# The last two row tiles' transposes on the DMA queue, and a group copy ahead of the seventh exponential, in a GroupNorm attention kernel

## What is computed

```python
h = group_norm(x, gn_w, gn_b); hf = h.reshape(B, C, H * W)        # (8, 128, 1024)
q = einsum('bcn,oc->bno', hf, wq) + bq
k = einsum('bcn,oc->bon', hf, wk) + bk[None, :, None]
v = einsum('bcn,oc->bno', hf, wv) + bv
alpha = softmax(einsum('bnc,bcm->bnm', q, k) / sqrt(C), axis=-1)   # (8, 1024, 1024)
out = einsum('bnm,bmc->bnc', alpha, v)
out = einsum('bnc,oc->bon', out, wo) + bo[None, :, None]
return out.reshape(x.shape) + x
```

## Time and profile before

| | us |
|---|---|
| median of 3 runs | 223.59 |
| lowest and highest | 222.37, 223.93 |
| the profiled execution | 222.1 |
| its span | 220.4 |
| TensorE busy (matmuls) | 203.2 |
| VectorE busy | 180.9 |
| ScalarE busy | 177.3 |
| GpSimd busy | 166.3 |

### The profile page before, as it was taken

The page is one execution under the profiler, slowest core; times in us unless marked ns, Lnnn a source line. Parts: engine busy times, 40 slices in busy tenths (PEclk is TensorE's granted clock), DMA queues, the critical chain, the costliest instruction groups (busy, mean ns, idle before and its releaser), DMA issues.

```text
span 220.4 us, 4306 instructions
## 1 busy us (share of the span) xinstructions
PE 203.2 (92%) x1513; PEld 139.9 (63%) x1513; DVE 180.9 (82%) x277; ACT 177.3 (80%) x279; POOL 166.3 (75%) x233
## 2 busy tenths in 40 slices
PE   0898679999999999999999999999999989998993
PEld 0764236767576756767576766667576657765993
DVE  1788999988889887989889897989877887788642
ACT  2259989998888889888998699888998888888820
POOL 6039996876889979997889949999689986795500
PEclk9999999999999999999999999999999999999999
DMA  5790999999999999999999999999999999999981
GB/s 160 231 400 18 190 161 225 188 179 226 201 204 195 229 171 212 247 178 189 202 174 249 187 224 212 229 174 223 209 171 219 182 227 196 187 192 205 276 304 51
DMA packets 135029, 44.61 MB, mean 202 GB/s; under 512 B 131168, under 2 KB 131936, under 8 KB 135008
## 3 DMA queue, kind: packets, MB, share of 16 engines
q1 hardware_dynamic: 134432, 44.08, 102.0%
q10 hardware_dynamic: 576, 0.26, 0.4%
HBM read 7.61 MB, written 4.22 MB: 54 GB/s over the span
## 4 chain that ended last, share of the span: by engine, by line
PE 75%; DVE 9%; issue 8%; ACT 5%; DMA 2%; SPq 0%; ACTq 0%; DVEq 0%
PE O L601 11%; PE O L603 10%; PE O L602 10%; PE S L570 10%; PE S L574 10%; PE S L572 10%; DVE neg_logits L911 5%; PE M L467 3%; PE M L466 3%; PE M L468 3%; DVE parts L927 2%; DMA x_sb<-in_x_dram 2%; ACT S L779 2%; ACT av L759 2%; ACT parts L790 1%
## 5 line engine op out<-in xcount | busy, mean ns | idle before, releaser
L911 DVE TENSOR_SCALAR_CACHE_REDUCE neg_logits<-S,c_tok 128x1024 f32<-128x1024 f32 x64 | 81.9, 1280 | 22.7 <-PE S L574 22.4
L779 ACT ACTIVATE S<-neg_logits,exp_bias 128x1024 f32<-128x1024 f32 x64 | 71.6, 1118 | 17.9 <-DVE neg_logits L911 17.7
L927 DVE SCALAR_TENSOR_TENSOR parts<-S,parts 128x1024 f16<-128x1024 f32 x64 | 78.0, 1219 | 1.7 <-ACT parts L790 1.3
L601 PE MATMUL O<-pT,v_hi 128*128 128x256 f16 x240 | 65.3, 272 | 3.7 <-ACT av L759 3.7
L790 ACT ACTIVATE parts<-S 128x1024 f16<-128x1024 f32 x64 | 65.4, 1022 | 1.6
L603 PE MATMUL O<-pT,v_lo 128*128 128x256 f16 x240 | 65.4, 272 | 0.0
L602 PE MATMUL O<-pT,v_hi 128*128 128x256 f16 x240 | 65.4, 272 | 0.0
L570 PE MATMUL S<-h_hi,u_hi 128*128 128x512 f16 x128 | 38.1, 379 | 2.4 <-DVE parts L927 2.4
L574 PE MATMUL S<-h_hi,u_lo 128*128 128x512 f16 x128 | 38.1, 379 | 0.0
L572 PE MATMUL S<-h_lo,u_hi 128*128 128x512 f16 x128 | 38.1, 379 | 0.0
L601 PEld LDWEIGHTS O<-pT,v_hi 128*128 128x128 f16 x240 | 24.3, 101 | 11.2 <-issue 4.9
(11 more groups left out here) (148 smaller groups left out, 287.4 us busy)
## 6 DMA issues: line engine op xcount, KB each, us to landing
x_sb<-in_x_dram SPq DMA_DIRECT2D x7, 512.0 KB, 8.4
inv_rows<-inv_line SPq DMA_DIRECT2D x6, 512.0 KB, 4.8
out_dram<-x_sb SPq DMA_DIRECT2D x6, 512.0 KB, 3.8
pT<-parts SPq DMA_TRANSPOSE x62, 4.8
out_dram<-x_sb SPq DMA_DIRECT2D x3, 256.0 KB, 4.7
x_sb<-in_x_dram SPq DMA_DIRECT2D x2, 256.0 KB, 3.9
out_dram<-x_sb SPq DMA_DIRECT2D x2, 128.0 KB, 1.9
inv_line<-row_inv SPq DMA_DIRECT2D x6, 4.0 KB, 2.0
```

The lines of the kernel that those rows point to most:

```text
L601: nc.tensor.matmul(o, vh, ph, start=(m == 0), stop=False)
L779: nc.scalar.activation(S[T % 3][:, :], neg_logits[:, n % 2, :], ACT.Exp, scale=-1.0, bias=exp_bias[:, p, n:n + 1], accum_out=row_sum[:, p, ...
L911: nc.vector.tensor_scalar(neg_logits[:, n % 2, :], S[T % 3][:, :], c_tok[:, p, n:n + 1], None, ALU.add, ALU.min, accum_out=exp_bias[:, p, ...
L927: nc.vector.scalar_tensor_tensor(out=parts[:, T % SPLITS, N:2 * N], in0=S[T % 3][:, :], scalar=P_SCALE, in1=parts[:, T % SPLITS, 0:N], op0 ...
```

## The change

Two things. First, `transpose` is issued for all 64 tiles; `last_transpose` on TensorE, the copies behind it on ScalarE and VectorE and their semaphores go, and each half of `last_values` waits for the DMA transposes of its two tiles. Second, at n = 6 ScalarE's copy of the group sums moves from behind the tile's exponentials to ahead of them.

```diff
@@ sync
             for b in range(B):
                 for n in range(TILES):
-                    if TILES * b + n < LAST_TILES[0]:
-                        transpose(b, n)
+                    transpose(b, n)
@@ tensor: last_values
                 if half == 0:
                     pe.wait_ge(inv_out, I0 + 3)
-                    for t in range(GT // 2):
-                        pe.wait_ge(tr_in[GT + t], 16 * B)
                 else:
                     pe.wait_ge(lo_done, TILES * B - 2)
-                    pe.wait_ge(last_tr_hi, 2)
-                    pe.wait_ge(last_tr_lo, 2)
+                for t in range(GT // 2):
+                    pe.wait_ge(tr_in[GT + 2 * half + t], 16 * B)
@@ tensor
-            def last_transpose(T):
-                pe.wait_ge(lo_done, T + 1)
-                for m in range(2 * TILES):
-                    done = nc.tensor.transpose(S[T % 3][:, :].bitcast(fp16)[:, m * 128:(m + 1) * 128],
-                                               parts[:, T % SPLITS, m * 128:(m + 1) * 128], ident16[:, :])
-                done.then_inc(last_tr, 1)
@@ tensor: behind the loop
                 if n == 1:
                     spread_inverse(I0 + 2, 1, B - 1, 0)
-                    last_transpose(LAST_TILES[0])
                 if n == 2:
-                    last_transpose(LAST_TILES[1])
                     spread_inverse(I0 + 3, 2, B - 1, 1)
                 values(*unit_of(B, n))
@@ scalar
+                    if n == 6 and b >= 1:
+                        copy_values(b - 1, 1)
                     exponentials(b, n)
                     if n == 2 and b >= 1:
                         copy_values(b - 1, 0)
-                    if n == 6 and b >= 1:
-                        copy_values(b - 1, 1)
                     high_part(b, n)
             copy_inverses(I0 + 2)
-            for i, T in enumerate(LAST_TILES):
-                act.wait_ge(last_tr, i + 1)
-                nc.scalar.copy(last_pT(T)[:, 0:TILES, :], ...).then_inc(last_tr_hi, 1)
             copy_inverses(I0 + 3)
@@ vector
-            for i, T in enumerate(LAST_TILES):
-                dve.wait_ge(last_tr, i + 1)
-                nc.vector.tensor_copy(last_pT(T)[:, TILES:2 * TILES, :], ...).then_inc(last_tr_lo, 1)
```

More of the change, by code:

```diff
@@ L120, in groupnorm_attention_kernel @@
         ident_ready = sem("ident_ready")
-        last_tr, last_tr_hi, last_tr_lo = sem("last_tr"), sem("last_tr_hi"), sem("last_tr_lo")
         a_mm, small_mm, ob_mm, woT_mm, b_mm = (
@@ L178, in groupnorm_attention_kernel @@
         I0 = 0
-        LAST_TILES = (TILES * B - 2, TILES * B - 1)
         LAST = (slice(0, GT // 2), slice(GT // 2, GT))
@@ L191, in groupnorm_attention_kernel @@
         LAST_INV = last_inv[:, 2:4, :].rearrange("c q n -> c (q n)")
-        def last_pT(T):
-            return pT[:, T // GT % PT, :, T % GT, :]
         def unit_of(b, n):
@@ L837, in _ @@
                         copy_values(b - 1, 0)
-                    if n == 6 and b >= 1:
-                        copy_values(b - 1, 1)
                     high_part(b, n)
             copy_inverses(I0 + 2)
-            for i, T in enumerate(LAST_TILES):
-                act.wait_ge(last_tr, i + 1)
-                nc.scalar.copy(last_pT(T)[:, 0:TILES, :],
-                               S[T % 3][:, 0:HALF].bitcast(fp16).rearrange("p (m n) -> p m n", m=TILES)
-                               ).then_inc(last_tr_hi, 1)
             copy_inverses(I0 + 3)
@@ L997, in _ @@
             low_part(B - 1, TILES - 1)
-            for i, T in enumerate(LAST_TILES):
-                dve.wait_ge(last_tr, i + 1)
-                nc.vector.tensor_copy(last_pT(T)[:, TILES:2 * TILES, :],
-                                      S[T % 3][:, HALF:N].bitcast(fp16).rearrange("p (m n) -> p m n", m=TILES)
-                                      ).then_inc(last_tr_lo, 1)
             dve.wait_ge(xres_done, B)
```

## The result

The changed kernel takes 224.33 us (median of 19 runs) against 222.92 us of the kernel before on the same chip: a ratio of 1.0053, 95% interval 1.0028 to 1.0077. I had forecast 219.2 us, 4.4 us faster; it is 1.2 us slower by the ratio, 1.4 by the medians. The run profiled here took 225.28 us, with a span of 223.5. Medians are over all runs; ratios are formed from the fast runs alone, those within 1.5% of the kernel's fastest.

The account below looks back on a forecast made before the run. TensorE was taken to set the pace, with the DMA engines the second candidate. Closed holes 4.1 us plus tail 0.3 us made 4.4 us, so 219.2 us for the median from 223.59; range 217.5 to 221.3.

Parts of the forecast that it names:

- The holes: TensorE's main loop: seven waits on ScalarE's group-sum copy, 0.66 us five times and 0.80 twice, 4.9 us, would close entirely.
- the delay of the exponential: ScalarE at n=6: exp(6) starts 0.61 us later behind the moved copy; taken to cost nothing on the path.
- Taken off all engines alike: Tail estimate: the six earlier holes, 4.1 us, subtracted from the old trace's times on all engines alike.
- Two transposes: Tail: tiles 62 and 63 move from TensorE, freeing 1.8 us there, to SP's queue; tail wins 0.3 us.
- The stores become the end: Tail: stores queued behind tile 63's transpose, 6.6 us of data, set the end; last landing 219.6 against 219.9.
- Two: Rival in the tail, 12%: last transpose lands late, at 215.5; 2.1 us lost of the 4.1 won, 221.6 us.
- 213.5: Tail sign: TensorE would be the better place for the transposes only if the landing is past some 213.5.
- Three: Rival in the main loop, 9%: exp(6)'s delay reaches TensorE, up to 0.61 us per batch; median 222.7 us.
- four: Rival at n=6, 4%: bank O completes later than row_max, so the copy's wait delays everything; 226.0 us.
- Five: Rival before the last half, 3%: TensorE's wait drops its clock to 1.2 GHz, 24 matmuls take 2.6 us more; 221.1.
- the slower side: Whole run: the chance given to a result slower by more than about 1%, 2.2 us, was 0.04.

Follow-up runs that it names:

- the copy alone: Kernel before with only the group copy moved ahead of the exponential at n=6: 220.23 us, ratio 0.9806; with four of six spreads cut to 8 partitions, 218.34 us.
- load taken off or moved: Changed kernel with four of six inverse-row spreads writing 8 partitions, not 128 (219.03 us), or with stores of batches 0 to 2 behind all transposes (223.01 us).
- the transposes alone: Kernel before with tiles 62 and 63 transposed by the DMA queue, copy left behind the exponential, holes left in: 223.77 us, ratio 1.0040.
- the changed kernel run again: The changed kernel, unaltered, measured a second time beside the kernel with 14 extra matmuls: 224.14 us, ratio 1.0043.
- the late stores: Stores of batches 0 to 2 put behind all transposes, in the kernel with only the copy moved (218.01 us) and in the changed kernel (223.01 us).
- the shifted stream: Changed kernel with 64 one-column matmuls ahead of the first projection, shifting TensorE's instruction stream by 128 instructions: 226.96 us in a single run.

## Why the prediction was wrong

**The holes (seven, 4.9 us): right.** They were where I saw them, closed for the reason given, and the delay of the exponential cost TensorE nothing: relieved of the queue's lag the copy alone wins 4.7 us from tile 0.

**"Taken off all engines alike": wrong, and this is the step that failed.** I worked out the tail on the clock of the trace before and took 4.1 us off everything, SP's queue included. That queue has a pace of its own. It was behind from tile 27 on and never quite caught up. I had the sign in hand, as tile 61 went out 0.8 us after its data and the DMA row stood at nine tenths. I read the lag only at the last tile, where it has shrunk: the last batch has no spreads and no stores between its transposes. At tile 41 it was 3.8 us. Forecast from tile 0, tile 63 should have gone out at 188.5; it went out at 193.6 in the changed kernel and at 193.4 with the holes left in. So the closed holes brought the transposes nothing. With the load taken off or moved it goes out at 188.2 and 188.4, where the forecast had it. Where the last transposes stay on TensorE the holes do pay, 2.6 us or more: the step failed because the change puts the tail behind the very queue that had not followed.

**Two transposes: one term mis-sized.** I gave tile 62 2.3 us of SP's time (205.96 to 208.3), and the same for tile 63 frees SP at 210.7. They take 3.0 to 3.2 each. A part of this is one stop of the transposes for 1.2 us beside an instruction packet; another is that 2.3 was the value of one transpose, where the 62 of the trace before hold SP for 1.4 to 4.0 us, 2.6 in the median. With the holes left in, the forecast has SP free at 210.7 - 15.7 = 195.0 from tile 0; in the transposes alone it is at 196.6. These 1.6 us turn my 0.3 us of gain into a loss of about 1 us, which the transposes alone show (0.9 by the ratio, 1.1 from tile 0 in the trace).

**The stores become the end: right in kind.** From SP free of tile 63 (210.7) to the last landing (219.6) the forecast has 8.9 us; it is 8.7 in three traces, and 9.4 in the one whose end the slow clock sets.

The misses add up on the trace. From tile 0 the forecast has the last landing at 219.6 - 15.7 - 4.1 = 199.8, and it is 206.2, 6.4 us later: 5.1 in the issue of tile 63 (193.6 against 188.5, of which 4.1 is the gain that was not passed on), 0.8 in the time that it holds SP (3.2 against 2.4), 0.5 behind it. The run profiled is one of the slower ones; in the changed kernel run again the last landing is at 205.1, 5.3 us later than forecast.

**The rivals.** Two came nearest: tile 63 lands at 198.8 from tile 0, later than its 195.7 (215.5, less 15.7 and 4.1). On the forecast's clock that is 218.6, far past the 213.5 at which I had said that TensorE would be the better place. But I gave as cause a slow transpose, and the cause is a late issue. Three and four did not happen: the copy waits for bank O and starts within 0.04 us of it. Five happened, and I had given it 3%: the changed kernel's TensorE was granted half clock from 216.7 on, 1.0 us after it had resumed behind a wait of 3.0 us. The stretches (us, PE busy, PEld, DVE, ACT, POOL, clock, DMA share, GB/s):

```profile
212.50:215.70 3.20, 0.17 (x2) 0.02 (x1) 0.85 (x2) 0.00 (x0) 0.00 (x0) 1.00 0.81 216
215.70:216.70 1.00, 0.99 (x10) 0.90 (x11) 0.00 (x0) 0.00 (x0) 0.00 (x0) 1.00 1.04 426
216.70:220.00 3.30, 3.30 (x17) 2.10 (x14) 0.00 (x0) 0.00 (x0) 0.00 (x0) 0.50 1.02 405
```

It cost the matmuls 1.5 us and this run some 0.7, and the run again shows the same wait without it. Not one of my rivals was that the queue does not follow, though the earlier trace rows named the DMA engines as the second candidate. That the slower side got 4% came of that.

## What to carry to other kernels

A hole in the busiest engine is worth closing only as far as every queue behind it keeps up: measure the lag from "data ready" to "transfer issued" for transfers all along the run, not for the last one, before taking a gain as passed on. A queue that runs behind in the middle is not seen while its results are needed late, and its lag comes due at the first place where the next step waits at once, here in the tail. Work that nobody waits for, like early stores, should leave such a queue while it is behind, if it does not then stand in front of something that is waited for: the late stores fit the copy alone (218.0 us) and not the change (223.0).

## What the runs showed of the hardware

DMA transposes stood still for about 1.2 us when a 16 KB instruction packet came by: median landings of 5.9 against 4.7 us in the trace of the changed kernel, 5.3 to 6.0 against 4.5 to 4.8 over all traces. The stop moved when TensorE's instruction stream was shifted.

TensorE's clock, in the traces with a wait before the last half: behind a wait of 3.04 us (the changed kernel) it fell to its 1.2 GHz level 1.0 us after matmuls had started again, and the last 15 of 24 matmuls ran at 0.21 us each instead of 0.11. Behind one of 2.25 us (the shifted stream) it fell after 0.3 us. Behind one of 3.01 us (the changed kernel run again) and one of 1.85 us (the transposes alone) it did not fall before the last matmul was over. So the same kernel with the same wait had it and had it not. With fourteen matmuls into an unused tensor in the wait, the last 24 ran at the full clock.
